# A two-layer attention and FFN kernel: the third and fourth output tile of the first attention move to the banks of the scores

## The reference

```python
x = x + _L0_xattn_ref(_layernorm(x), ctx, ctx, mask, wq, wk, wv, wo)
# in it, after the rotary embedding of q and k:
scores = jnp.einsum('bhgqd,bhkd->bhgqk', qg, k) / scale
masked = jnp.where(mask[:, None, None].astype(bool), scores, -1000000000.0)
w = jax.nn.softmax(masked, axis=-1)
out = jnp.einsum('bhgqk,bhkd->bhgqd', w, v)
return out.transpose(...).reshape(bs, s, N_Q_HEADS * D_V) @ wo
```

## Time and profile before

| | |
|---|---|
| runs (3) | 2485.04, 2485.53, 2486.96 us |
| median | 2485.53 us |
| span of the profiled execution | 2485.7 us |
| TensorE matmuls, busy | 2381.5 us (96%) |
| VectorE, busy | 1630.6 us (66%) |
| ScalarE, busy | 1256.1 us (51%) |
| GpSimd, busy | 1226.5 us (49%) |
| output tiles of both layers, L854 | 689.4 us in 3072 matmuls of 381 ns |
| X additions of both layers, L2123 | 188.3 us in 256 instructions of 747 ns |

### The profile page before, as it was taken

One profiled execution on the slowest core, in us unless ns is written; L12 is line 12 of the kernel. 1 busy time (PEld: TensorE's weight loads), 2 busy tenths in 40 slices (PEclk: granted clock), 3 DMA queues, 4 the chain that ended last, 5 costly groups with the idle time before them and its releaser, 6 DMA issues.

```text
span 2485.7 us, 45205 instructions
## 1 busy us (share of the span) xinstructions
PE 2381.5 (96%) x17711; PEld 1307.3 (53%) x17719; DVE 1630.6 (66%) x3133; ACT 1256.1 (51%) x2425; POOL 1226.5 (49%) x981
## 2 busy tenths in 40 slices
PE   7699999999999999999999999999999999999998
PEld 4355555555555555544444555555555655555554
DVE  6877777777777778765443555666666666655666
ACT  6665555555555554532323464555455545544443
POOL 3556656666666666423322255454454444445541
PEclk9899999999999999999999999999999999999999
DMA  6111111111111111102010101122212212211101
GB/s 205 26 43 35 52 42 45 35 44 35 44 35 43 35 27 45 26 9 68 26 32 15 43 8 41 27 63 56 54 44 52 51 45 60 52 42 27 26 14 68
DMA packets 221554, 108.16 MB, mean 44 GB/s; under 512 B 174080, under 2 KB 197280, under 8 KB 221344
## 3 DMA queue, kind: packets, MB, share of 16 engines
q1 hardware_dynamic: 221344, 105.27, 16.7%
HBM read 61.62 MB, written 4.19 MB: 26 GB/s over the span
## 4 chain that ended last, share of the span: by engine, by line
PE 58%; POOL 17%; DVE 9%; ACT 5%; issue 5%; DMA 0%; DVEq 0%; POOLq 0%; ACTq 0%
PE PB L854 13%; PE PB L806 13%; PE PB L966 9%; POOL AR L2681 6%; PE PB L790 6%; PE PB L983 5%; POOL AR L2686 4%; POOL PSP L2699 3%; PE PB L896 3%; PE PB L831 3%; DVE X L2123 2%; PE PB L762 2%; DVE AR L2108 1%; ACT JUNK L1316 1%; POOL AR L2676 1%
## 5 line engine op out<-in xcount | busy, mean ns | idle before, releaser
L854 PE MATMUL PB<-WB,AR 128*128 128x512 f16 x3072 | 689.4, 381 | 13.2 <-DVE X L2123 8.8
L806 PE MATMUL PB<-XTB,WB 128*128 128x512 f16 x3072 | 683.7, 380 | 3.4 <-ACT WB L1352 1.9
L854 PEld LDWEIGHTS PB<-WB,AR 128*128 128x128 f16 x3072 | 296.3, 98 | 374.4 <-DVE X L2123 20.0
L806 PEld LDWEIGHTS PB<-XTB,WB 128*128 128x128 f16 x3072 | 299.1, 98 | 343.6 <-issue 5.3
L2692 POOL TENSOR_TENSOR AR<-AR,SML 128x512 f32<-128x512 f32 x128 | 144.6, 1151 | 316.7 <-DVE SML L2093 316.7
L2123 DVE SCALAR_TENSOR_TENSOR X<-PB,SML,X 128x512 f32<-128x512 f32 x256 | 188.3, 747 | 163.0 <-PE PB L854 156.5
L1476 ACT ACTIVATE AR<-PB 128x512 f16<-128x512 f32 x256 | 132.3, 602 | 266.1 <-PE PB L896 266.1
L1974 DVE TENSOR_TENSOR AR<-AR 128x512 f16<-128x512 f32 x128 | 138.3, 1080 | 110.6 <-ACT AR L1392 110.2
L2681 POOL TENSOR_TENSOR AR<-AR,CST 128x512 f32<-128x512 f32 x128 | 181.8, 1421 | 44.2 <-ACT AR L1386 44.2
L2003 DVE TENSOR_TENSOR AR<-PB,AR 128x512 f16<-128x512 f32 x128 | 88.1, 690 | 170.4 <-ACT AR L1439 170.4
L966 PE MATMUL PB<-XTB,AR 128*128 128x512 f16 (+1 forms) x864 | 192.5, 379 | 0.0
(11 more groups left out here) (272 smaller groups left out, 3745.7 us busy)
## 6 DMA issues: line engine op xcount, KB each, us to landing
STG<-in_wo SPq DMA_DIRECT2D x14, 1024.0 KB
STG<-in_wq SPq DMA_DIRECT2D x13, 1024.0 KB
STG<-in_qw_gu SPq DMA_DIRECT2D x40, 128.0 KB
STG<-in_ctxT SPq DMA_DIRECT2D x4, 1024.0 KB
X<-in_x SPq DMA_DIRECT2D x4, 1024.0 KB, 9.8
out_x<-X SPq DMA_DIRECT2D x16, 256.0 KB, 2.4
AR<-PSP SPq DMA_TRANSPOSE x240, 2.4
STG<-in_wk SPq DMA_DIRECT2D x14, 256.0 KB
```

The costliest lines, as they stand in the source:

```text
L806: m = pe.do.matmul(b[:, :], wq[x][:, k, h * 128:(h + 1) * 128], XT[y][c][:, k, :], start=n == 0, stop=n == 11)
L854: m = pe.do.matmul(b[:, :], AT[x][:, h, t * 128:(t + 1) * 128], wo[y][:, h, :], start=n == 0, stop=n == 11)
```

## The change

In the first attention, for output units 0 to 29 (worked on in turns 1 to 30 of the loop), output tiles 2 and 3 are written into banks 4 and 5, those of the scores, in place of banks 0 and 2. Both TensorE's `output` and VectorE's X addition ask the new function `out_bank`. Output units 30 and 31, which `turn_over` works on, and the whole second attention keep 2, 3, 0, 2. The waits follow from `bank`; no instruction other than waits is added, removed or moved.

```diff
-        QB, WB_OUT, PVB = (0, 1, 6, 7), (2, 3, 0, 2), ((0, 1), (6, 7))
+        QB, PVB = (0, 1, 6, 7), ((0, 1), (6, 7))
+
+        def out_bank(L, u, t):
+
+            return ((2, 3, 4, 5) if L == 0 and u < NU - 2 else (2, 3, 0, 2))[t]
...
-                b = bank(WB_OUT[t], (x_add, (L, u, t)))
+                b = bank(out_bank(L, u, t), (x_add, (L, u, t)))
...
-                dve.do.scalar_tensor_tensor(xs, PB[WB_OUT[t]][:, :], co(L, u, 0), xs, ALU.mult, ALU.add
+                dve.do.scalar_tensor_tensor(xs, PB[out_bank(L, u, t)][:, :], co(L, u, 0), xs, ALU.mult, ALU.add
                                             ).then_inc(x_add.of((L, u, t)), 1)
```

## The result

| | before | after |
|---|---|---|
| median (lowest to highest), 15 runs each | 2485.95 (2485.04 to 2488.97) us | 2490.79 (2487.61 to 2491.76) us |
| span of the profiled execution | 2485.7 us | 2488.3 us |
| VectorE's last low half ahead of the end of unit 29 is done (L1974; after: L1978) | 991.92 us | 986.50 us |
| first `unpack_d` matmul behind tile 3 of output unit 30 (L949; after: L953) | 1057.90 us | 1063.78 us |

The account below looks back on a forecast made before the run. It took a ring through TensorE, ScalarE, GpSimd and VectorE as the bound, VectorE's queue holding it in 13 unit ends. Gains of 10.5 us less losses of 8.3 took 2.2 off 2485.7; median forecast 2483.4, range 2477.5 to 2490.

Parts of the forecast that it names:

- the 512-wide ends: Thirteen unit ends behind a 512-wide weight or context preparation: VectorE's queue stays as long, so gain 0 each.
- the 256-wide ends: Six unit ends behind a 256-wide preparation: L2676 can start 0.35 us earlier, then L1953 holds it; 2.1 us together.
- the clock in unit 29: Pauses around `unpack` could lower TensorE's clock, 1.7 us more; left out of the sum, kept as bound.
- Three kinds of ends: Unit ends sorted by preparation, 512-wide (13), 256-wide (six) or none (five), and by what L2676 waits for last.
- the ring: A unit's dependency loop: TensorE's keys, ScalarE's half turns, GpSimd's rotation, queries, VectorE's last low half, X additions, TensorE again.
- the whole bubble: Rival: TensorE is the bound, its waits of 40.6 and 8.8 us vanish, only 8.3 are paid: 2444; chance 0.04.
- a renamed wait: Rival: `weigh` waits for the DMA transposes of P in all ends; no gains, losses stay: 2493.8; chance 0.03.
- No preparation, 0.97 each: Ends of units 4, 11, 15, 19, 23: `weigh` and scores 1.39 us earlier, L2676 0.97 earlier; 4.9 us together.
- Units 1, 2, 27, 28, 3.5: The other ends: gains of 1.0, 0.35, 1.1 and 1.05 us from waits of `weigh` removed, together 3.5.
- Unit 29, 3.1: `unpack` waits for X addition 2 and tile 3 for L2207, so tile 3's X addition ends later: loss 3.1 us.
- Unit 30, 5.2: The same stall around `unpack`: loss 3.5 us at full clock, plus 1.7 for a clock fall behind a 5.6 us pause.
- Rival 4: Slower: stalls around `unpack` cost 10.0 with the clock down in both, gains stay under 5: 2491.6; chance 0.12.

Follow-up runs that it names:

- the first kernel: The changed kernel with output units 28 and 29 (ends of units 29 and 30) kept on banks 0 and 2: 2480.33 us against 2486.52 before, ratio 0.9974.
- the kernel that took 2476.28 us: Against the kernel before, new banks only in ends 1, 2, 4, 11, 15, 19, 23, 27, 28 and ten 512-wide ends, no 256-wide: 2476.28 us against 2486.34, ratio 0.9962.

## Why the prediction was wrong, step by step

The prediction failed at three terms: the 512-wide ends put at nothing, the gain of the 256-wide ends, and the clock in unit 29, which it left out.

- *Three kinds of ends, and who holds the ring in each*: right for before. GpSimd's idling for VectorE in half of the ends was the decisive view, and the rivals that promised the whole bubble, or only a renamed wait, did not happen.
- *No preparation, 0.97 each*: right by itself (0.99), though not in how L2672 is slowed. "GpSimd gets on by about a fifth of the time in which L2050 runs" is not what the rows show: it ended 2.41 to 2.42 us behind the start of the pair whether it began 0.02, 0.33 or 0.61 us behind it (2.39, 2.09 and 1.80 us), that is 1.13 us behind the pair's end, so it had done 0.14 us of its 1.27 at most by then, wherever it began. By that the gain would be 0.9; the pair came 0.99 us earlier and not 0.90. In the whole change four of the five gave 0.43 to 0.57, since TensorE came in late. What failed is the silent step that TensorE would be ready at VectorE's mark.
- *512-wide, "13 x 0, what the scores lose would be hidden up to 2.0 us"*: this failed. The wait ahead of `weigh` became two pauses, 1.35 to 1.5 and 0.8 to 1.0 us. Behind them TensorE ran at the granted clock of 0.50, the keys ended 1.34 us later against VectorE's mark (unit 18: 8.30 instead of 6.96), and L2676 then fell on other VectorE work and took 2.12 instead of 1.27. That used up the 2.0 us and took TensorE's lead from the free end. Filling the pauses gave it all back. The prediction looked for a fall of the clock only around `unpack`; "1.39 us of idling do not [lower it]" was true of one pause and was used where there are two in a row. Its sign for being wrong, VectorE idle in a 512-wide end, would have missed this: TensorE held the ring and VectorE had other work.
- *256-wide, 0.35 each*: wrong sign, +0.15. The step assumed that L1953 stays where it is when L2672 comes earlier (0.66 us, against VectorE's mark). But L2672 now starts ahead of VectorE's pair L2050 and slows it by 0.50 us. The prediction had used the Trainium skill's rule on the shared port only for GpSimd as the loser ("SBUF — State Buffer", "SBUF: two separate sides"). The rule speaks of whoever comes second: by it the pair gets nothing until GpSimd is done at 628.43 and ends 1.28 later, at 629.71; the trace has 629.58. So the trace agrees with it to 0.13 us. Units 26 and 27 speak for the port as the cause: where the pair reads PSUM, GpSimd overlaps it by 0.67 and 0.81 us, and each takes the 1.27 to 1.28 us that it takes without overlap. No run was made to try it.
- *Units 1, 2, 27, 28, 3.5*: measured 3.65, of which the 0.87 of unit 1 is luck: kernels that leave unit 1 as it was have it too. Units 2, 27 and 28 gave 2.8 where 2.5 was forecast.
- *Unit 29, 3.1*: the stall was exact, 3.08. The term of the clock, put at nothing and kept as a bound of 1.7, was 2.5: the whole of tile 3 at half the clock. In the kernel with units 29 and 30 alone changed it was 1.7.
- *Unit 30, 5.2*: measured 5.5, with 3.58 as the stall and 2.0 as the clock. The prediction took the fall of before to be paid for in its 1034.0, but it cost nothing: in the first kernel the same pause of 2.77 us is followed by a `weigh` of 1.48 us and not 2.75, and the next output tile starts 6.94 us behind VectorE's mark all the same (before: 6.97), since it waits for L2112.
- *The sum*: gains 5.4 instead of 10.5 (1.2 of them luck, the -0.3 and unit 1), below their bound of 6; losses 11.3 instead of 8.3, above theirs of 10. Of the gains that are missing 3.1 belong to the 256-wide ends and 2.4 to the clock in the 512-wide ends and behind them; of the added losses 2.5 are the clock in unit 29. Rival 4 (slower, 2491.6: small gains and the clock down in both stalls) is the nearest to what happened. Its price is summed wrongly: it takes off 2.1, the gain of the 256-wide ends that it puts at nothing, where the 3.5 of units 1, 2, 27 and 28 belongs; with that it is 10.0 - 1.8 - 3.5 = +4.7, 2490.2. Rival 4 had the 256-wide ends giving nothing and the collision of L2672 with VectorE as the cause, but placed that in the free ends, where it costs only what the forecast had allowed. The 0.2 us between span and median compared two things: the time of a run lies 1.8 us above its span (after: 2490.13 and 2488.3). That doesn't bear on the verdict.

## What to carry to other kernels

When a buffer change removes a wait, write down where the engine will stand idle next, and whether one pause has become two short ones: on TensorE that can cost the clock, even if the idle time itself is hidden. Ask of each place in a loop by itself whether the early start is of use; here 18 of 30 unit ends pay by the traces (ten of them by only 0.10 us), and the version that picks them and unit 1 is 0.38% faster than before while the blanket one is 0.17% slower. And look who else uses the new banks: two four-matmul broadcasts, each between two tiles, cost twice what the 28 ends ahead of them had given.

## What the runs showed of the hardware that was not expected

- The granted clock fell to 0.50 behind two pauses of about 1.35 and 0.97 us with 0.86 us of scores between them, in 12 of the 16 ends of 512-wide units that had them in all the kernels here. It did not behind 0.6 and 0.97 us (none of the ten such ends in the kernel of the 512-wide ends alone, units 6, 10, 14, 18 and 22, and the same five in the kernel that took 2476.28 us), and not in any of the five filled ones. The end of unit 8 had the long pair in four kernels and fell in one only. What decides there is open. So it is with one pause of 2.77 us ahead of `weigh` in unit 30: its 24 matmuls took 2.75 us in the kernel before and 1.48 in the first kernel.
- Where VectorE's pair of subtractions and GpSimd's rotation overlap and both read SBUF alone, the one that starts second pays. GpSimd second, by 0.02 us: 2.39 us for its own 1.27, VectorE's pair 1.28. VectorE second, by 0.64: its pair 1.78, GpSimd's 1.27. An operation that comes half a microsecond earlier can so delay the critical one. Where the pair reads PSUM the overlap costs neither anything: 1.27 and 1.28 us in unit 26, with GpSimd 0.60 us behind it in the changed kernel and 0.54 ahead in the kernel before.
- A pause of 2.3 us, four short matmuls and a pause of 1.6 us put the next 5 us at half the clock, in a place where before there was no pause and no fall.
